# Convolution block: the packed rows' store, VectorE's order and the squares' order

## The reference, cut to what matters

```python
x = x + L0_conv(_gn(x))            # the block of this case
t = t + L1_attn(_ln_t(t)); t = t + L1_ffn(_ln_t(t))
# inside L0_conv, per image, heads of 12 channels:
q, k = q/norm(q), k/norm(k)
o = 0.5*v + einsum(q, einsum(k, v))/pi;  o = o/norm(o)
o = (o + silu(layernorm(xs) @ fc1) @ fc2) @ proj
```

## Time and profile before

| | before |
|---|---|
| median of 3 runs | 2925.92 us (2918.25 to 2927.51) |
| profiled execution | 2920.95 us |
| its span | 2919.2 us |
| granted TensorE clock, mean | 0.972 |
| PE / DVE / ACT / POOL busy | 93% / 79% / 67% / 39% |

### The profile page before, as it was taken

How to read it: one execution, slowest core, us unless ns; L and a number is a source line. 1 busy time by engine, 2 the same in 40 slices (tenths; PEclk the granted TensorE clock), 3 DMA queues, 4 the chain that set the end, 5 groups by cost and what they waited for, 6 DMA issues and landing times. The chain is left out here.

```text
span 2919.2 us, 93533 instructions
## 1 busy us (share of the span) xinstructions
PE 2710.1 (93%) x32934; PEld 1668.9 (57%) x32934; DVE 2306.5 (79%) x4651; ACT 1967.2 (67%) x3559; POOL 1151.7 (39%) x1999
## 2 busy tenths in 40 slices
PE   4899999999998489999999999999999997899996
PEld 2555555555554256666666666666666664455553
DVE  3576676767666489999999999999999994678997
ACT  2677677776766257777777777777777774577775
POOL 0153434434344444444444444444444441224445
PEclk9999999999998789999999999999999998999998
DMA  1113232332332366666666666666666664334555
GB/s 34 42 57 108 83 113 81 108 103 86 113 108 70 123 125 119 117 117 117 117 117 117 117 117 117 117 117 117 117 117 117 117 117 90 98 100 134 147 142 153
DMA packets 945258, 316.21 MB, mean 108 GB/s; under 512 B 852193, under 2 KB 934402, under 8 KB 945154
## 3 DMA queue, kind: packets, MB, share of 16 engines
q1 hardware_dynamic: 943810, 313.61, 48.1%
q10 hardware_dynamic: 1344, 1.18, 0.1%
HBM read 113.35 MB, written 99.88 MB: 73 GB/s over the span
## 5 line engine op out<-in xcount | busy, mean ns | idle before, releaser
L1032 DVE TENSOR_REDUCE at_unit_max<-at_ps_queries 128x1 f32<-128x512 f32 (+4 forms) x2304 | 1134.9, 549 | 86.3 <-PE at_ps_queries L903 83.8
L978 ACT ACTIVATE at_probs<-at_ps_keys 128x512 f32<-128x512 f32 x1344 | 743.6, 604 | 387.9 <-PE at_ps_keys L918 383.4
L903 PE MATMUL at_ps_queries<-at_turned 96*128 96x128 bf16 (+3 forms) x3456 | 634.2, 274 | 32.1 <-DMA at_turned<-at_spread 31.3
L918 PE MATMUL at_ps_keys<-at_turned 128*128 128x128 bf16 (+3 forms) x3456 | 648.5, 275 | 2.0 <-ACT at_probs L978 1.7
L853 POOL TENSOR_TENSOR at_v<-at_stacks,at_one 128x128 f32<-128x128 f32 x192 | 76.6, 399 | 820.9 <-DMA at_stacks<-qkv_rows 820.9
L938 PE MATMUL at_ps_values<-at_probs,at_v 128*32 128x128 f32 x10752 | 373.4, 276 | 6.4 <-ACT at_probs L978 6.4
L918 PEld LDWEIGHTS at_ps_keys<-at_turned 128*128 128x128 bf16 x3456 | 237.5, 97 | 240.4 <-ACT at_probs L978 88.8
L903 PEld LDWEIGHTS at_ps_queries<-at_turned 96*128 96x128 bf16 x3456 | 289.2, 97 | 123.1 <-DMA at_turned<-at_spread 32.9
L938 PEld LDWEIGHTS at_ps_values<-at_probs,at_v 128*32 128x32 f32 x10752 | 269.5, 109 | 120.4 <-ACT at_diag_probs L978 70.2
L606 PE MATMUL cb_ps_hidden<-cb_xn_t,fc 96*128 96x512 f32 x384 | 196.4, 636 | 57.8 <-ACT cb_hidden_t L540 57.8
L978 ACT ACTIVATE at_diag_probs<-at_ps_keys 128x512 f32<-128x512 f32 x384 | 208.6, 595 | 8.3 <-PE at_ps_keys L918 5.3
(11 more groups left out here) (212 smaller groups left out, 4778.3 us busy)
## 6 DMA issues: line engine op xcount, KB each, us to landing
qkv_rows<-cb_packed SPq DMA_DIRECT2D x32, 1536.0 KB, 5.8
at_stacks<-qkv_rows SPq DMA_DIRECT2D x192, 256.0 KB, 3.3
cb_x<-in_x_dram SPq DMA_DIRECT2D x32, 384.0 KB, 3.9
cb_x_again<-in_x_dram SPq DMA_DIRECT2D x128, 96.0 KB, 3.5
x_after_conv<-cb_x SPq DMA_DIRECT2D x128, 96.0 KB, 2.5
attention_rows<-at_att SPq DMA_DIRECT2D x384, 32.0 KB, 2.2
ff_att_rows<-attention_rows SPq DMA_DIRECT2D x32, 384.0 KB, 4.5
ff_x<-x_after_conv SPq DMA_DIRECT2D x128, 96.0 KB, 2.3
```

Of the source, the lines that this page charges most:

```text
L903: mm = pe.matmul(pq[:, u % QBANKS, c0:c0 + n], QT[0:STACK, slot, qb * P:(qb + 1) * P], KT[0:STACK, slot, k0:k0 + n], start=(c0 == 0), stop ...
L918: mm = pe.matmul(pk[:, bank_k, c0:c0 + n * P], KT[:, slot, kb * P:(kb + 1) * P], QT[:, slot, q0 * P:(q0 + n) * P], start=(c0 == 0), stop=True,
L978: act.activation(probs, pk[:, (slot * NU + k) % KBANKS, :], ACT.Exp, scale=scale).then_inc(S["probs"], 1)
L1032: dve.tensor_reduce(peaks, scores, AX.X, ALU.max).then_inc(S["unit_max"], 1)
```

## The change

Four edits, all in `conv_block`:

```diff
@@ SP
-                    if on(7):
-                        sp.wait_ge(S["low_ready"], i - 6)
-                        sp.dma_start(rows[i - 7].rearrange(...), PK[:, (r + 1) % 2, ...]
-                                     ).then_inc(rows_stored[(r + 1) % 2], 16)
-                _pipeline(sp, body, BATCH, 8, 2, ahead=1)
+                    if on(6):
+                        sp.wait_ge(S["low_ready"], i - 5)
+                        sp.dma_start(rows[i - 6].rearrange(...), PK[:, r, ...]
+                                     ).then_inc(rows_stored[r], 16)
+                _pipeline(sp, body, BATCH, 7, 2, ahead=1)
@@ VectorE: the query matrix's copy goes behind the low part
-                    if on(2):
-                        dve.wait_ge(S["m_done"], i - 1)
-                        dve.tensor_copy(MM[:, :], M_).then_inc(S["m_ready"], 1)
                     if on(5):
...
                     if on(6):
...
+                    if on(2):
+                        dve.wait_ge(S["m_done"], i - 1)
+                        dve.tensor_copy(MM[:, :], M_).then_inc(S["m_ready"], 1)
@@ VectorE: the sums' order
-                        dve.wait_ge(S["squares"], 2 * i)
-                        dve.tensor_reduce(VS[:, :], SQ[:, :, 2 * C:3 * C], AX.X, ALU.add)
+                        dve.wait_ge(S["squares"], 2 * i - 1)
                         dve.tensor_reduce(NS[:, :, :], SQ[:, :, 0:2 * C]...,
-                                          AX.X, ALU.add).then_inc(S["norm_sums"], 1)
+                                          AX.X, ALU.add)
+                        dve.wait_ge(S["squares"], 2 * i)
+                        dve.tensor_reduce(VS[:, :], SQ[:, :, 2 * C:3 * C], AX.X, ALU.add).then_inc(S["norm_sums"], 1)
@@ ScalarE: the square of q and k comes ahead of that of x
+                        act.activation(SQ[:, :, 0:2 * C], QKV[:, q, :, 0:2 * C], ACT.Square).then_inc(S["squares"], 1)
                         act.activation(SQ[:, :, 2 * C:3 * C], ...)
-                        act.activation(SQ[:, :, 0:2 * C], QKV[:, q, :, 0:2 * C], ACT.Square).then_inc(S["squares"], 1)
```

More of the change, by code:

```diff
@@ L395, in body @@
                                          ).then_inc(x1_stored[r], 16)
-                    if on(7):
-                        sp.wait_ge(S["low_ready"], i - 6)
-                        sp.dma_start(rows[i - 7].rearrange("(t p) n -> p t n", p=P),
-                                     PK[:, (r + 1) % 2, :, :].rearrange("p (t j) n -> p t (j n)", j=HEADS)
-                                     ).then_inc(rows_stored[(r + 1) % 2], 16)
-                _pipeline(sp, body, BATCH, 8, 2, ahead=1)
+                    if on(6):
+                        sp.wait_ge(S["low_ready"], i - 5)
+                        sp.dma_start(rows[i - 6].rearrange("(t p) n -> p t n", p=P),
+                                     PK[:, r, :, :].rearrange("p (t j) n -> p t (j n)", j=HEADS)
+                                     ).then_inc(rows_stored[r], 16)
+                _pipeline(sp, body, BATCH, 7, 2, ahead=1)
                 for r in range(2):
```

## The result

The changed kernel takes **2887.48 us** (median of 4 runs, 2887.08 to 2889.93) against 2923.74 for the kernel before: ratio 0.9879, 95% interval 0.9861 to 0.9897. Forecast: 2903, range 2884 to 2918; the measured time lies 3.5 us inside the range's lower end. The profiled executions stand 33.9 us apart in their spans (2919.2 and 2885.3).

A forecast was written before the change was run, and what follows sets the result against it. TensorE's repeated wait at L606 for the first silu was taken as the bound. Gains of 3.4, 7.4, 2.6, 3.5 and 6.4 (23.3 us) took 2920.95 to 2897.6; adding 5.0 for the median gave 2903 us, range 2884 to 2918.

The forecast's parts named there:

- The store's wait and v: GpSimd: v no longer waits for the store, so every round has v delay VectorE's low part to about 3.03 us.
- The new gap of `out_sums`: TensorE waits for the query matrix ahead of `out_sums`: 1.38 us in odd rounds, 1.16 in even ones.
- Rival 1: VectorE: v doesn't delay the low part, `out_sums` waits for nothing; 2866 us, chance 0.07.
- Ordinary and long gaps: TensorE's gaps ahead of L606: 20 ordinary rounds gain 3.4 us, seven rounds with long gaps 7.4.
- the sum: All terms together: 23.3 us off the profiled 2920.95, so 2897.6 for such an execution.
- Start: Rounds 1 to 4: VectorE starts after the first square instead of waiting for both; 2.6 us gained.
- Run-out: Round 35: the high part no longer waits for the store, with later work behind it; 3.5 us gained.
- The clock: TensorE's clock falls behind gaps, 1.6 us each: eight counted, four taken as removed, 6.4 us gained.
- Rivals 2 and 4: Clock falls as often as now: 2909, chance 0.13; falls behind the new gap in nearly every round: 2939, chance 0.06.
- Rival 3: Gain given back behind L606, or store was hidden; only the ends' 6 us stay: 2920, chance 0.12.
- From one execution to the median: Whole kernel: the median of runs is 5.0 us above the profiled execution, taking 2897.6 to 2903.

The follow-up runs named there:

- e_store: The kernel before with only the store moved to the round of the low part: 2972.38 us, ratio 1.0163.
- e_v_late: The changed kernel with v on GpSimd waiting for the low part of the round ahead of it, not for the scale alone: 2852.14 us, ratio 0.9751.
- e_no_squares: The changed kernel with the squares and their sums in the old order: 2889.26 us, ratio 0.9881.
- e_gap_short: The kernel `e_v_late` with one spare reduction (0.87 us) on VectorE ahead of the sums: 2886.25 us.
- e_gap_double: The changed kernel with two spare reductions (0.87 us each) on VectorE ahead of the query matrix's copy: 2975.15 us.

## Why the prediction was right, and where its size was off

- **The store's wait and v.** Right: v's wait for the store is gone, and v stands between q and k and the low part in every round. `e_store` and `e_v_late` show both sides of it. The 5.8 us given for the store's landing are a median (5.7 to 7.5 before); it changed nothing, as neither v nor the high part waits for it now.
- **The new gap of `out_sums`.** Right in kind; 1.21 and 1.07 us where 1.38 and 1.16 were forecast, with rounds of 27.57 and 27.43 for 27.6 and 27.4. Rival 1, the low part not delayed, is what `e_v_late` builds by moving v: its 2866 for the changed kernel's own order did not happen.
- **Ordinary and long gaps.** From round 5 to round 32 the seven falls of before (7 x 1.6 = 11.2 us) account for half of the 21.6. The other 10.4 stand against 8.1 in the sum: 3.4, and 5.9 for six long gaps, less 1.2, since round 32's new gap lies in this stretch and its old one behind it.
- **Start.** 3.4 for 2.6; `e_no_squares` has 2.9 of it for the squares' order.
- **Run-out.** The high part of round 35 starts at 955.81 as q and k end, with no wait for a store. The 10.3 us are 3.6 of that, for 3.5 in the sum; 2.8 of round 32's old gap and 1.6 of its fall; and 2.4 of matrix products at another clock than before. `out_sums` of round 33 took 4.51 us and now 2.80, L606 there 3.62 and 3.28, the last attention rows 4.08 and 3.12; against it, `out_sums` of round 34 took 3.94 and now 4.53.
- **The clock: the term that was mis-sized.** I took four falls of eight to stay (6.4 us gained). None stayed: 12.8, and 2.4 more in the run-out, 8.8 of the 10.6 us by which the spans moved further than forecast. I had counted falls by rounds and not asked how they thin out with the gap's length, though the earlier trace rows and the ordinary rounds already stood for two points of that curve. Rivals 2 and 4 are out: gaps of 1.2 us brought no fall. Rival 3 is out too, as the rounds themselves got shorter.
- **From one execution to the median.** The sum's 2897.6 stands against the profiled 2887.08. The forecast added 5.0 us, the distance of the median from the profiled execution before; the changed kernel's median lies only 0.4 above its profiled one. That is 4.6 of the 15.5 us between 2903 and 2887.48, and no fault of the mechanism.

The Trainium skill's rule ("SBUF — State Buffer", section "Who interferes with whom") held in each trace: VectorE's operations with two inputs in SBUF and GpSimd's, which read SBUF, waited each other out, in whichever order they came, while reductions on VectorE ran their normal 0.94 and 1.74 us beside GpSimd's work.

## What to carry to other kernels

Before a wait is taken off one engine, ask what that wait kept it from colliding with: an operation that was late by accident may have been hidden by it, and moving it on purpose (one semaphore wait moved, `e_v_late`) can be worth as much again as the change (35 us behind 36). Work out both chains that end at the critical engine, since the gain of each edit is cut off where the other begins. And count what TensorE's clock loses behind its gaps: from round 5 to round 32 the shorter gaps saved 11.2 us through the clock and 10.4 by themselves.

## What the runs showed of the hardware that I had not expected

In these traces the clock's falls depend steeply on the gap: none behind 51 gaps of 1.07 to 1.23 us (the changed kernel's and e_gap_short's), 16 behind 73 of about 1.5 to 1.7, 44 behind 48 of 2.8 to 2.9. A fall mostly cost 1.2 to 1.6 us; one round of `e_gap_double` lost 2.6, and two of `e_store` 3.3.
